# Row normalisation of a gated attention and expert layer: GpSimd writes the normalised rows in place of VectorE

## The reference

```python
x = x + tanh(g_xattn) * attention(layernorm(x), ctx, ctx)   # 16 heads of depth 8
x = x + tanh(g_ffn) * experts(layernorm(x))                 # 8 experts, top 2 by a router, hidden width 256
layernorm(x) = (x - mean(x)) / sqrt(var(x) + 1e-5)          # over the 128 features of a row
```

## Time and profile before

| what | us |
|---|---|
| median of 3 runs | 640.82 |
| lowest and highest of them | 636.71, 643.01 |
| the execution that was profiled | 636.26 |
| its span, first to last instruction | 634.5 |

### The profile page before, as it was taken

How to read it: one execution, slowest core, us unless ns; L and a number is a source line. 1 busy time by engine, 2 the same in 40 slices (tenths; PEclk the granted TensorE clock), 3 DMA queues, 4 the chain that set the end, 5 groups by cost and what they waited for, 6 DMA issues and landing times.

```text
span 634.5 us, 18476 instructions
## 1 busy us (share of the span) xinstructions
PE 547.3 (86%) x6201; PEld 393.0 (62%) x6213; DVE 367.2 (58%) x1361; ACT 363.2 (57%) x835; POOL 264.8 (42%) x281
## 2 busy tenths in 40 slices
PE   2359989888889899989989999989998869999996
PEld 1124555555555566766657667656776658898875
DVE  3345778678878865444785555586544424324364
ACT  5214866665656666566565656566565546656441
POOL 6030100100177101445374544574535557676771
PEclk9986999999899999999999999999999979999999
DMA  4353556455456367764298554465433336685441
GB/s 127 100 142 85 145 144 166 91 145 150 91 168 185 64 128 100 169 117 140 65 182 120 146 101 118 144 129 125 109 93 104 80 89 164 150 151 157 110 110 54
DMA packets 158121, 78.65 MB, mean 124 GB/s; under 512 B 85088, under 2 KB 153312, under 8 KB 158032
## 3 DMA queue, kind: packets, MB, share of 16 engines
q1 hardware_dynamic: 119760, 45.65, 33.4%
q10 hardware_dynamic: 31104, 17.13, 9.9%
q0 software_dynamic: 7168, 14.69, 9.6%
HBM read 30.72 MB, written 36.75 MB: 106 GB/s over the span
## 4 chain that ended last, share of the span: by engine, by line
PE 58%; DVE 12%; DMA 10%; issue 8%; ACT 6%; SPq 3%; POOL 2%; ACTq 1%; DVEq 0%; POOLq 0%
PE y L607 12%; PE bank_oT L517 6%; DMA q_st<-q_dram 6%; PE scores L503 6%; DVE neg_max L1028 4%; PE hidden_p L591 4%; PE max_scores L482 4%; PE hidden_p L592 3%; PE max_scores L541 3%; ACT probs L744 2%; PE hidden_p L593 2%; PE bank_oT L648 2%; PE o L530 2%; PE o L648 2%; ACT hidden L810 2%
## 5 line engine op out<-in xcount | busy, mean ns | idle before, releaser
L1028 DVE TENSOR_REDUCE neg_max<-max_scores 128x4 f32<-128x308 f32 x244 | 116.0, 475 | 133.6 <-PE max_scores L482 129.4
L744 ACT ACTIVATE probs<-scores 77x512 f32<-77x512 f32 x256 | 148.7, 596 | 48.4 <-PE scores L503 45.8
L1365 POOL DMA_INDIRECT xs_dram<-rows,at x112 | 109.7, 980 | 81.2 <-PE max_scores L482 49.7
L1380 POOL DMA_INDIRECT back<-ys_dram,at x112 | 107.6, 961 | 61.5 <-PE max_scores L482 25.3
L517 PE MATMUL bank_oT<-probs,v_cols 77*9 77x128 f32 x2048 | 103.8, 278 | 9.2 <-ACT probs L744 8.0
L503 PE MATMUL scores<-q_st,k_st 128*77 128x128 bf16 x1024 | 105.7, 228 | 0.2
L503 PEld LDWEIGHTS scores<-q_st,k_st 128*77 128x77 bf16 x1024 | 72.3, 118 | 46.6 <-issue 39.3
L482 PE MATMUL max_scores<-k_st,q_st 128*128 128x308 bf16 x244 | 74.9, 307 | 28.8 <-DMA q_st<-q_dram 14.5
L810 ACT ACTIVATE hidden<-hidden_p,b_cols 128x128 f32<-128x128 f32 x256 | 73.5, 372 | 43.1 <-PE hidden_p L593 37.2
L607 PE MATMUL y<-w_sb,hidden 128*128 x608 | 92.3, 290 | 0.0
L607 PEld LDWEIGHTS y<-w_sb,hidden 128*128 128x128 f32 x608 | 81.0, 194 | 2.2
(11 more groups left out here) (144 smaller groups left out, 906.5 us busy)
## 6 DMA issues: line engine op xcount, KB each, us to landing
ys_dram<-ys ACTq DMA_DIRECT2D x38, 256.0 KB
q_st<-q_dram SPq DMA_DIRECT2D x16, 512.0 KB
k_st<-k_dram SPq DMA_DIRECT2D x64, 77.0 KB
xs_all<-x SPq DMA_DIRECT2D x16, 256.0 KB, 4.2
q_dram<-q_hl SPq DMA_DIRECT2D x16, 256.0 KB
xs_dram<-zeros_b ACTq DMA_DIRECT2D x16, 256.0 KB, 3.3
out<-xs_all SPq DMA_DIRECT2D x16, 256.0 KB
k_dram<-k_hl SPq DMA_DIRECT2D x48, 77.0 KB
```

The costliest lines, as they stand in the source:

```text
L744: nc.scalar.activation(probs[h][:], score_bank[h % 2][0:KEYS, :], ACT.Exp, scale=SCALE).then_inc(s_exp, 1)
L1028: V.tensor_reduce(neg_max[:, i // 2, :, h, i % 2], max_to(b, h)[:, 0:PER * KEYS].rearrange("p (j k) -> p j k", j=PER), AXIS_X, ALU.max, ne ...
L1365: G.indirect_dma_start(out=xs_dram[c % 2], out_offset=bass.IndirectOffsetOnAxis(ap=at[k][c % 4][:, i:i + 1], axis=0), in_=rows[c % 2][:, i ...
L1380: G.indirect_dma_start(out=back[k][:, b % 16, :], out_offset=None, in_=ys_dram[c % 2][0:TILES[c] * 128, :], in_offset=bass.IndirectOffsetO ...
```

## The change

`normed1` and `normed2` move from DVE's program into POOL's, with the same four instructions each, now on GpSimd. `normed1(u - 1)` stands directly behind `rstd1_of(u - 1)` (slot with r = 0, DVE had it in the slot with r = 1), `normed2(u - 4)` directly behind `rstd2_of(u - 4)` (r = 2, before r = 3), both ahead of the slot's scatters and gathers. The waits go along: for the root, for the transposition of the group before (`p_xT1`, `p_xT2`), for `rows_low` of the group before; `normed2` gets one more, for the attention of the group's four sequences (`s_x1`). The semaphores that PE, ACT and DVE wait on are the same.

```diff
@@ DVE @@
-            def normed1(g):
-                dve.wait_ge(s_rstd1, g + 1)
-                if g:
-                    dve.wait_ge(p_xT1, g)
-                for i in range(NB):
-                    V.tensor_scalar(xn1[:, i, :], xs_all[:, NB * g + i, :], mv1[g % 2][:, i, 0:1],
-                                    rstd1[g % 2][:, i:i + 1], ALU.subtract, ALU.mult).then_inc(s_xn1, 1)
...
-            def normed2(g):
-                dve.wait_ge(s_rstd2, g + 1)
-                if g:
-                    dve.wait_ge(p_xT2, g)
-                    dve.wait_ge(s_rlo, clip(g, G0))
-                for i in range(NB):
-                    V.tensor_scalar(xn2[:, i, :], xs_all[:, NB * g + i, :], mv2[g % 2][:, i, 0:1],
-                                    rstd2[g % 2][:, i:i + 1], ALU.subtract, ALU.mult).then_inc(s_xn2, 1)
...
-                if r == 1 and group_on(u - 1):
-                    normed1(u - 1)
...
-                if r == 3 and group_on(u - 4):
-                    normed2(u - 4)
@@ POOL @@
+            def normed1(g):
+                pool.wait_ge(s_rstd1, g + 1)
+                if g:
+                    pool.wait_ge(p_xT1, g)
+                for i in range(NB):
+                    G.tensor_scalar(xn1[:, i, :], xs_all[:, NB * g + i, :], mv1[g % 2][:, i, 0:1],
+                                    rstd1[g % 2][:, i:i + 1], ALU.subtract, ALU.mult).then_inc(s_xn1, 1)
+
+            def normed2(g):
+                pool.wait_ge(s_x1, NB * (g + 1))
+                pool.wait_ge(s_rstd2, g + 1)
+                if g:
+                    pool.wait_ge(p_xT2, g)
+                    pool.wait_ge(s_rlo, clip(g, G0))
+                for i in range(NB):
+                    G.tensor_scalar(xn2[:, i, :], xs_all[:, NB * g + i, :], mv2[g % 2][:, i, 0:1],
+                                    rstd2[g % 2][:, i:i + 1], ALU.subtract, ALU.mult).then_inc(s_xn2, 1)
...
                 if r == 0 and group_on(u - 1):
                     rstd1_of(u - 1)
+                    normed1(u - 1)
                 if r == 2 and group_on(u - 4):
                     rstd2_of(u - 4)
+                    normed2(u - 4)
```

## The result

The change makes the kernel slower by 0.8%: a median of 646.38 us against 641.65 us before, twenty executions each, ratio 1.0078 with a 95% interval of 1.0052 to 1.0104. That is some 5.0 us (0.0078 x 641.65). By the prediction's bound of one per cent it is no clear change, but it is on the other side of the forecast (2.5 us faster), and 646.38 lies just outside the range, which ended at 646.

The account below looks back on a forecast made before the run. PE was busiest (86%), with DVE short of room in some stretches; gain is limited to PE's waits for DVE. Terms -3.0 + 0.1 + 0.4 = -2.5 us took 640.82 to 638.3 us, range 631 to 646.

Parts of the forecast that it names:

- d: Time of one row-normalising instruction on POOL: taken as 0.30 us, nearest to the affine select, with ends 0.19 and 1.04.
- the bound of 0.51: First scatters: with d under 0.51 us, no rows come late for PE's transposition there.
- The formula for the start: First group's rows, ahead of PE's first transposition: the move costs 4d - 1.11, 0.1 us at d = 0.30.
- The formula for the first scatters: POOL's 24 back-to-back DMAs: PE's transposition is late by 16d - 8.14; at d = 0.30, 3.3 us to spare.
- the gains: PE's shorter waits for DVE: 1.1 + 1.6 + 0.3 = 3.0 us; with collisions counted, 2.6.
- The wait for the DMA of q: PE's waits from 68 to 432 us for q, 5.1 us, which no engine's speed shortens; to stay some 5.
- The share of the router's rows: Rows of `normed2`, slot with r = 3: hidden behind the DMA of q and later PE; gain 0.3 us for all.
- Collisions: POOL and DVE holding each other up over SBUF: 0.4 us lost, bounds 0 and 9.6.
- What was costed at nothing: First scatters' DMAs up to 4.8 us later, and last gathers pushed back but regained from POOL's waits: no cost.
- B: Rival: POOL needs twice DVE's time, d = 0.69; start and first scatters late, 642.8 us, no change; chance 0.14.
- C: Rival: POOL is slow and becomes the bound, d = 1.04; start and first scatters late, 649.8 us; chance 0.12.
- A: Rival: DVE's lead adds up and its chain pieces come off in full, 9.5 us, giving 631.3 us; chance 0.16.

Follow-up runs that it names:

- experiment 9: Seven forms of POOL instruction, four of each, added to the kernel before at places with slack; full form 800 ns, product of two tensors 456 ns.
- experiment 3: The change with five groups' rows back on DVE (the first, four at the first scatters), 27 on POOL; ratio to before 0.9893, second run 0.9898.
- experiment 1: The change with only the first group's rows ahead of q back on DVE; 643.28 us, ratio to before 0.9998.
- both runs of 7: The change with two wide two-tensor instructions a group on POOL instead of four, all 32 groups; 648.80 and 648.93 us, ratios to before 1.0110 and 1.0143.
- experiment 4: The kernel before, rows still on DVE, plus 27 x 4 POOL instructions of the same form into a scratch tile; 642.43 us, ratio 0.9995.
- experiment 2: The change with only the four groups among the first scatters back on DVE; 637.95 us, ratio to before 0.9947.
- experiment 8: Five groups' rows on DVE, the other 27 on POOL as two wide two-tensor instructions each; 643.64 us, ratio to before 1.0001.

## Why the prediction was wrong

**The step that failed is the price of POOL's instruction**: "I take d = 0.30, nearest to the affine select". Measured: 0.79. The bounds, 0.19 and 1.04, held it; the choice between them did not. The three rows near the lower end were a memset, a select and one input pair's subtraction *per column of a wide instruction*. The last, 0.236 for 128 columns, was carried from a 1024-column instruction by its width alone, and a product of two 128-column tensors measured 0.456 in experiment 9: what an instruction costs whatever its width was missing. None of the rows had two operations or took scalars from a tile. The one row that had arithmetic on a small tile, the power's 1.04, was nearer to the truth than all the cheap ones. And the subtraction of 1.885 us has two inputs; DVE's own, of the same width, takes 1.22. That made POOL 1.5 times as slow as DVE, and d 0.43 to 0.53 (from 1.11 / 4 and from the mean of 0.346 on DVE), at the bound of 0.51 and not at 0.30.

**The formula for the start was right.** 4d - 1.11 makes 2.05 at d = 0.79; the first transposition came 2.09 us later. What it left out stands one group on. The second group's transposition in before, in the change and in experiment 3 (second run):

```profile
31.61 1.09 PE L448 MATMUL group<-ident,xn 128*128 128x128 f32 x4 [1.51 <-DVE xn L976]
```

```profile
31.75 1.04 PE L448 MATMUL group<-ident,xn 128*128 128x128 f32 x4
```

```profile
29.57 0.60 PE L450 MATMUL group<-ident,xn 128*128 128x128 f32 x4
```

There PE waited 1.51 us for DVE's rows, ahead of the 68 us from which the prediction read its waits. On POOL that wait is gone: the change is only 0.14 us late there, and experiment 3 is 2.0 us early. This gain was not in the sum; what it is worth in time no run shows by itself.

**The formula for the first scatters was right in place, and short in size.** The bound "d < 0.51" was passed, and the transposition named did wait. 16d - 8.14 makes 4.5 us at d = 0.79; the waits for rows there are 3.35 and 2.53, 5.9 in all, since two groups are late and not one. With the terms of the prediction the sum at the measured d is 2.05 + 4.5 - 2.6 = +3.95 us, against some +5.0 measured: the mechanism holds, and one price carries the wrong sign. That the sum comes so near is in part luck. The places cost 11.7 us and not 6.55, the gains are 6.7 and not 2.6, and the two errors cancel.

**The gains were there, and larger in time than in waits.** I summed 3.0 us from PE's waits; in experiment 3 those waits shrink by 2.5 for 27 of 32 groups, but the time by 6.7, with an interval of about 4 to 9. The wait for the DMA of q, which should have stayed at 5.1, is 4.4 there (3.5 in the change). The share of the router's rows was probably put too low. A good part of the remainder goes with the clock: the mean over executions is 0.957 for before, 0.952 for the change and 0.965 for experiment 3. Over all executions with a clock on record a fit with one slope for all kernels gives 4.0 us for each 0.01 of mean granted clock; at equal clock the change stands 1.7 us above before and experiment 3 some 3.6 below, 5.3 us apart, near to the 6.55 (2.05 + 4.5) that the two formulas make. That fewer waits raise the clock and that the rest follows so is consistent with these numbers and with the stretches shown above. From 200 to 236 us the mean granted clock is 0.81 or 0.86 in the four profiles in which PE waits there for rows (the change, experiment 1 and both runs of 7), and 0.86 to 1.00 in the nine others. But no run here forced the clock, and a stretch at the lower level comes without such a wait too (experiment 4 has the 0.86; the 1.06 us of the transposition at 212.87 in experiment 2 lies in one), so it is not shown.

**Collisions** were taken at 0.4 us and are nearer to nothing: `rows_low` went from a mean of 682 to 698 ns, 14 times 0.016, and experiment 4 shows no cost of the whole. The bound of 9.6 was far off for this form; for the form with two tensors experiment 8 shows that it can happen.

**What was costed at nothing** was nothing: the later scatters release no wait of PE, elsewhere the rows arrive in time at 3.1 us a group, and behind 240 us the distance between the two traces stays between 8.2 and 10.7 us up to the end, where it is 10.0.

**The rivals.** B had the right kind and nearly the right price, d = 0.69 for 0.79, and its 642.8 was "no change"; its sum put half a per cent less on the time than came. C, which loses from d = 0.59 on through the start and the first scatters, is what happened, at a smaller price than its 1.04: its mechanism is shown by experiments 1 to 3, but not that POOL becomes the bound elsewhere (experiment 4). A, the chain's pieces in full, is not excluded by the time of experiment 3 alone; at equal clock the 3.6 us are far from its 9.5. B and C, in which the kernel loses time, held 0.26 of the chance, and the row that should have raised it stood in the earlier trace rows. The Trainium skill, "GPSIMD Engine Reference", section 4.1, says that GpSimd is roughly at line rate with one input. The trace does not agree for this form, which has one tensor as input: 800 ns, 2.3 times DVE's 346. A copy took 283; no run has one of that shape on DVE to compare.

## What to carry to other kernels

Before work is moved to another engine, price it by a row with the same form, operations and width on that engine; a rate taken from a wide instruction hides what each instruction costs by itself, and where no such row exists, the expensive bound deserves as much weight as the cheap one. Then look for the few places where the receiving engine has no slack (its first piece in a line of dependent steps, and where its queue is full back to back) and leave those pieces where they were: five groups of 32 turned a loss of 0.8% into a gain of 1%. A late operand may cost more than the wait that it shows (here 11.7 us, give or take 3, for 8.0 us of waits), so a place is priced by putting it back.

## What the runs showed of the hardware that was not expected

- GpSimd's price is that of the form, 283 to 800 ns for the same 128x128 tile, with some 370 ns that do not depend on the width for the form used here (experiment 9).
- A two-tensor instruction of 512 columns on GpSimd holds up a two-input instruction on DVE in nine of ten meetings (0.68 us becomes 0.85 to 1.50); beside a one-tensor instruction it mostly stays at 0.68 (experiment 8).
- The granted clock of PE falls to 0.50 for stretches of 3.4 to 24 us in every execution profiled, at places that differ between them; before has some 29 us of them in its profiled execution, the change some 62 (mean granted clocks of 0.977 and 0.952 over 634.5 and 644.5 us). The executions of one kernel spread with it, those of before from 635.1 to 653.1, over more than the change is worth. Profiles of two kernels are therefore compared by places and by waits, and their times over many executions only.
